# A graph and attention block on one core: ScalarE's weight conversions placed elsewhere, the context in other PSUM banks, and an output product begun at half the context

## The reference

```python
xn = _layernorm(x, axis=-1)
x = x + gnn(xn, edge_index, ...) + mix(xn[None], w_qkv, w_out, b_out, ln_scale)[0]
x = x + ffn(_layernorm(x, axis=-1)[None], ...)[0]

def mix(x, w_qkv, w_out, b_out, ln_scale):            # 8 heads of 64
    q, k, v = jnp.split(jnp.einsum('bnc,cf->bnf', x, w_qkv), 3, axis=-1)
    q = jax.nn.softmax(q, axis=-1)                    # over a head's 64
    k = jax.nn.softmax(k, axis=1)                     # over the nodes
    context = jnp.einsum('bnhd,bnhe->bhde', k, v / N)
    out = jnp.einsum('bhde,bnhd->bhen', context, q / 8)
    out = jnp.einsum('bnf,fc->bnc', heads_joined(out), w_out) + b_out
    return layernorm(out) * ln_scale

def gnn(x, ...):                                      # two layers
    x = prelu(x @ lin_W.T + lin_b)
    agg = jax.ops.segment_sum(x[src], dst, num_segments=n)
    h = prelu((x + agg) @ W1.T + b1) @ W2.T + b2      # then batch norm and relu
```

## Time and profile before

| | us |
|---|---|
| median of 3 runs (530.35 to 535.58) | 530.47 |
| the profiled execution | 531.56 |
| its span, first to last instruction | 529.8 |
| TensorE busy | 478.6 |
| VectorE busy | 323.4 |
| ScalarE busy | 251.7 |
| GpSimd busy | 166.1 |
| mean granted TensorE clock | 0.960 of full speed |

### The profile page before, as it was taken

The page is one execution under the profiler, slowest core; times in us unless marked ns, Lnnn a source line. Parts: engine busy times, 40 slices in busy tenths (PEclk is TensorE's granted clock), DMA queues, the critical chain, the costliest instruction groups (busy, mean ns, idle before and its releaser), DMA issues.

```text
span 529.8 us, 10016 instructions
## 1 busy us (share of the span) xinstructions
PE 478.6 (90%) x3589; PEld 363.3 (69%) x3589; DVE 323.4 (61%) x737; ACT 251.7 (48%) x526; POOL 166.1 (31%) x176
## 2 busy tenths in 40 slices
PE   2989999997997997997999995999999978989893
PEld 1767558875764665664899993668999857866641
DVE  4667698746969855863453536644333376439777
ACT  4778334137451345153235553534336377743344
POOL 1469154003039103033124990002321323303502
PEclk9989999999999989998899997999999957999998
DMA  8602001200102002002100001000000295000015
GB/s 245 188 2 79 1 12 70 81 1 29 51 2 80 2 1 79 2 6 84 74 0 0 2 1 58 1 0 1 0 0 1 83 396 240 1 0 1 1 41 153
DMA packets 5245, 27.42 MB, mean 52 GB/s; under 512 B 1036, under 2 KB 1161, under 8 KB 3544
## 3 DMA queue, kind: packets, MB, share of 16 engines
q1 hardware_dynamic: 5208, 26.92, 14.7%
HBM read 24.36 MB, written 2.56 MB: 51 GB/s over the span
## 4 chain that ended last, share of the span: by engine, by line
PE 73%; DVE 13%; ACT 9%; issue 3%; POOL 1%; DMA 1%; SPq 0%; ACTq 0%; DVEq 0%
PE ps L454 45%; PE ps L612 17%; PE ps L443 5%; PE ps L704 2%; PE ps L508 2%; DVE r L1126 1%; PE ps L440 1%; ACT wslot L756 1%; DVE r L1578 1%; PE ps L518 1%; DVE stat L1148 1%; DVE r L1590 1%; POOL late L1631 1%; DVE r L1568 1%; ACT late L864 1%
## 5 line engine op out<-in xcount | busy, mean ns | idle before, releaser
L454 PE MATMUL ps<-r,wslot 128*128 128x250 f16 x840 | 97.7, 277 | 4.4 <-DVE r L1126 4.3
L454 PEld LDWEIGHTS ps<-r,wslot 128*128 128x128 f16 x840 | 83.1, 100 | 16.9 <-DVE r L1126 5.9
L612 PE MATMUL ps<-late,r 125*128 (+1 forms) x800 | 89.7, 274 | 3.8 <-issue 3.8
L612 PEld LDWEIGHTS ps<-late,r 125*128 125x128 f16 x800 | 78.8, 99 | 15.0 <-issue 4.5
L1639 POOL TENSOR_TENSOR wslot<-stage,wslot 128x512 f16<-128x512 f32 x32 | 39.4, 1261 | 155.7 <-ACT wslot L756 155.7
L454 PE MATMUL ps<-wslot,r 128*125 128x512 f16 x300 | 69.4, 382 | 0.0
L454 PE MATMUL ps<-wslot,late 128*125 128x512 f16 x240 | 56.3, 389 | 6.3 <-DVE late L1418 5.9
L1667 POOL TENSOR_TENSOR late<-ohs,late 128x250 f16<-128x250 f32 x40 | 25.6, 651 | 99.2 <-ACT late L929 99.2
L454 PEld LDWEIGHTS ps<-wslot,r 128*125 128x125 f16 (+1 forms) x300 | 39.4, 137 | 22.2 <-issue 2.3
L454 PE MATMUL ps<-late,wslot 128*128 x480 | 51.5, 270 | 0.0
L454 PEld LDWEIGHTS ps<-wslot,late 128*125 128x125 f16 x240 | 32.8, 140 | 25.2 <-issue 7.5
(11 more groups left out here) (181 smaller groups left out, 745.3 us busy)
## 6 DMA issues: line engine op xcount, KB each, us to landing
late<-in_tv SPq DMA_DIRECT2D x2, 4096.0 KB, 17.5
x<-in_x SPq DMA_DIRECT2D x5, 448.0 KB
out<-r SPq DMA_DIRECT2D x10, 224.0 KB
stage<-in_w_up SPq DMA_DIRECT2D x2, 1024.0 KB, 5.8
stage<-in_w_down SPq DMA_DIRECT2D x2, 1024.0 KB, 4.7
stage<-in_w_lin SPq DMA_DIRECT2D x1, 1024.0 KB, 6.5
stage<-in_w_k SPq DMA_DIRECT2D x1, 1024.0 KB, 4.8
stage<-in_w_q SPq DMA_DIRECT2D x1, 1024.0 KB, 4.9
```

Of the source, the lines that this page charges most:

```text
L454: last = nc.tensor.matmul(out, stat_(hs, b), mov(hm, b), start=start and n == 0, stop=stop and n == 3 * blocks - 1)
L612: last = nc.tensor.matmul(bank("t", m), u_nat[layer][:, p, h, m * 128:(m + 1) * 128], counts(h)[:, chunk], start=(start and h == 0 and p = ...
```

## The change

The arithmetic and the number of instructions stay. What moves:

- ScalarE's weight conversions. "v": from behind the exponentials to between the last two key windows. "out": scaled after q5's exponential, high half after q6's; before, both after v0's window copy. "down0": scaled after v4's window copy, high half after v5's; before, both after v9's. "up1": scaled after v8's window copy, high half at mix tile 0; before at mix tiles 2 and 3. "down1": mix tiles 4 and 5; before 6 and 7.
- The context's PSUM banks: z slots 2 and 3 in place of the two x banks.
- The products m 0 and m 1 wait for the first half of the context only.
- Windows: one of the five of the mix stage now stands between m 1 and m 2 (phase "ctx"), and the other four follow mix tiles 0 to 3 directly; before, five followed tiles 1 to 5.
- The slot of "q" counts as read after q9, not after the last value tile.

```diff
-WINDOWS = {"up0": 4, "k": 6, "v": 10, "mix": 5}
+WINDOWS = {"up0": 4, "k": 6, "v": 10, "ctx": 1, "mix": 4}
...
-    "z": [("qv", 2 * T, "dve", 0)],
+    "z": [("qv", 2 * T, "dve", 0), ("ctx", 2, "dve", 1)],
...
-READER = {"lin": ("t", "lin"), "up0": ("x", "up0"), "k": ("t", "k"), "q": ("z", "qv"), "v": ("z", "qv"), "out": ("n", "m"),
+READER = {"lin": ("t", "lin"), "up0": ("x", "up0"), "k": ("t", "k"), "q": ("z", "qv", QV.index(("q", T - 1)) + 1), "v": ("z", "qv"), "out": ("n", "m"),
...
             for b in range(2):
-                wait_bank(pe, "x", "ctx", b, b)
+                wait_bank(pe, "z", "ctx", b, 2 + b)
...
-            wait_done(pe, "x", "ctx", 2)
             for p in range(KB):
+                wait_done(pe, "z", "ctx", p // 2 + 1)
                 wait_bank(pe, "n", "m", p, p % 2)
...
+                if p == 1:
+                    window("ctx", 0)
...
-                if 1 <= t <= WINDOWS["mix"]:
-                    window("mix", t - 1)
+                if t < WINDOWS["mix"]:
+                    window("mix", t)
...
             for i in range(WINDOWS["k"]):
                 window("k", i)
+                if i == WINDOWS["k"] - 2:
+                    split_weight("v")
...
-            split_weight("v")
...
+                    if t == Q_FIRST - 2:
+                        scale_weight("out")
+                    if t == Q_FIRST - 1:
+                        high_weight("out")
...
                     window("v", t)
-                    if t == 0:
-                        split_weight("out")
-            split_weight("down0")
+                    if t in (4, 5):
+                        (scale_weight if t == 4 else high_weight)("down0")
+                    if t == T - 2:
+                        scale_weight("up1")
...
-                if t in (2, 6):
-                    scale_weight("up1" if t == 2 else "down1")
-                if t in (3, 7):
-                    high_weight("up1" if t == 3 else "down1")
+                if t == 0:
+                    high_weight("up1")
+                if t in (4, 5):
+                    (scale_weight if t == 4 else high_weight)("down1")
...
             dve.wait_ge(k_max, 2)
+            window("ctx", 0)
```

More of the change, by code:

```diff
@@ L1315, in _ @@
             dve.wait_ge(k_max, 2)
+            window("ctx", 0)
             for b in range(2):
-                wait_high(dve, "x", "ctx", b)
+                wait_high(dve, "z", "ctx", b)
                 for hh in range(2):
```

21 lines of the change are left out of this document (11 added, 10 removed).

## The result

The changed kernel took 535.77 us (median of 20 runs, 531.88 to 540.37), the kernel before 532.44 us (20 runs, 530.23 to 535.61). The ratio is 1.0055, with a 95% interval of 1.0037 to 1.0073: the change costs 2.9 us (2.0 to 3.9). This ratio, like those of the experiments, is an estimate over the runs with its interval, and not the quotient of the two medians (here 1.0063). The forecast of 529.6 us was a gain of 0.9 us, and 535.77 lies above its range, which ended at 533.5. Two of the missing 6.2 us are the level of the kernel before, whose median of 20 runs is 532.44 and not 530.47; the rest is the change.

What follows compares the result with a forecast made beforehand. TensorE was taken as the bound, busy 478.6 of 529.8 us. Terms -3.0 - 2.4 + 3.4 - 0.8 + 1.95 gave -0.85, say -0.9 us: 529.6 us from a median of 530.47, range 525.3 to 533.5.

Steps and rivals of the forecast that it cites:

- Step 1: Key stage: "v" converted in ScalarE's idle time; key transposes start at 126.65 instead of 129.69 us, 3.0 us earlier.
- Step 2: "out" converted between the queries: v1's 4.15 us stall goes, less dearer windows beside GpSimd; -2.4 us.
- the walk to v6: Value stage followed window by window: v6 starts on TensorE at 171.75 against 177.19 us, 5.4 us ahead.
- Step 3: "down0" and half of "up1" moved into the value stage: context at 192.75 us, 2.0 of 5.4 us left; +3.4 us.
- as in the mean: Price of a VectorE window beside GpSimd, from instruction times at 157 to 175 us: 4.1 us instead of 2.4.
- Steps 4 and 5: Context to end of mix tiles: -0.8 us up to mix 0, then +1.95 us in the mix tiles.
- Step 4: Context in the z pair, m begun at half: mix 0 15.5 us after the context's start, before 16.3; -0.8 us.
- Step 5: Mix windows without lag: each late, window 2 meets GpSimd's split of "up1" and costs 4.1 us; +1.95 us.
- TensorE's clock falls: Rival: two more falls to half speed behind late windows, turning -0.9 into +2.9 us, 533.4 us; 15 in 100.
- Every window waits in full: Rival: three full GpSimd waits per window, 5.8 us each; v0 to v2, v7, mix 2 add +8.5, 538 us; 3 in 100.

Runs made afterwards that it cites:

- e1: Kernel before with only the conversions of "v" and "out" moved as in the change; 527.83 us, ratio 0.9913 to the kernel before.
- e3: Changed kernel with "down0", "up1" and "down1" converted where they stood before; 524.45 us, ratio 0.9865 to the kernel before.
- e4: Changed kernel with each mix window one tile later again (lag restored); 534.43 us, ratio 1.0042 to the kernel before.
- e10: Changed kernel with GpSimd's split of "up1" held until all windows are built; 535.14 us, ratio 1.0024 to the kernel before.
- e2: Kernel before with only the context's banks, m begun at half, and the ctx and unlagged mix windows changed; 528.11 us, ratio 0.9944.
- e12: The same kernel as e3, run again in another batch; 524.71 us, ratio 0.9843 to the kernel before.
- e5: Changed kernel plus resultless matmuls: 8 before window v7, 5 before the context, 8 before mix window 2; 531.17 us, ratio 0.9992.
- e11: e3 with GpSimd's scaling of the ten query tiles held until all value windows are built; 519.34 us, ratio 0.9744 to the kernel before.
- e7: e6 with GpSimd's split of "down0" held until all ten value windows are built; 527.47 us, ratio 0.9898 to the kernel before.
- e6: e1 with the move of "down0" into the value stage added; 531.28 us, ratio 0.9964 to the kernel before.
- e9: e3 with both halves of "up1" converted at mix tile 0; 531.14 us, ratio 0.9985 to the kernel before.

## Why the prediction was wrong

- **Step 1 (-3.0).** Right: 126.44 for 126.65, no wait, ScalarE at 109.24 for 109.6.
- **Step 2 (-2.4) and the walk to v6.** Right: 171.50 for 171.75, with the dearer windows of v0 to v2 included. e1 gave 4.6 us as time.
- **Step 3 (+3.4): the step that failed.** The mechanism was the one described, and both waits for ScalarE came (1.98 and 3.44 us). But the term was mis-sized: some 6.0 us by the contexts of the seven profiles, 6.7 by after and e3. Of the 2.4 us that the context in after came later than forecast, 1.07 is window v7, for which I took 4.1 us "as in the mean", although a split of four instructions in a row was to lie right across it; it took 5.3, near the 5.8 that I had worked out for full waits. The mean of the earlier trace rows held windows that met the short scaling instructions, some of them in gaps, and was the wrong row for this place; it also left out the 125 x 2048 instruction, which can meet the split too. Another 1.05 is v9 at half clock, for which the term held nothing. Part of this is the execution's luck: in e4, the same program up to there, the window took 4.3 us, the clock did not fall and the context came 0.6 us late; in e10 it came 3.8 us late.
- **Steps 4 and 5 (-0.8 + 1.95).** Step 4 came to 15.9 us for 15.5. Step 5 was mis-assigned and mis-sized. The windows without lag are not all late, and cost no more than the missing fifth window saves (e2: 34.3 us against 34.7); what I had charged to them belongs to the split of "up1" in window 2 and the conversion ahead of it. That window took 4.8 us for 4.1, and the clock fell behind it (1.07 + 3.57 us for 0.62 + 2.75, so 1.27): together 38.2 us for 36.7.
- **The rival "TensorE's clock falls".** In the profile of after it is what happened, twice more than in before: at v9 and at mix tile 3. Its price, -0.9 turned to +2.9, is the measured 2.9. It had 15 in 100, because three late windows in before had passed at full clock, behind waits of 1.3 and 1.6 us that were no shorter than those of after. That row was weak evidence: e3 and e12 show that the same place of one program passes at full clock in one execution and falls in another. The agreement in the sum is partly luck: the two falls gave 2.3 us (1.05 and 1.27), against the rival's 1.9 each, and dearer windows 1.4. The Trainium skill (TensorE: Matmul & The Clock Gate, A second HAM failure mode) describes a kernel in which small pauses between groups of matmuls made the clock swing; here it fell behind pauses of 1.2 and 1.6 us, and stayed up at these two places when matmuls filled them (e5).
- **"Every window waits in full"** had 3 in 100 and was right for one window (5.3 us) and nearly for a second (4.8), not for all. The Trainium skill (SBUF — State Buffer, Who interferes with whom) calls the port pair an exclusive lock held for a whole instruction. Window v7 agrees: the 1 x 16 instruction that takes 0.15 us alone took 1.12, and ended with the split instruction beside it, which itself took 2.14 us for 1.16, because it had met the 125 x 2048 one.
- **The sum.** On the profile's own scale the forecast was 530.7 us; 2.4 at the context, 0.4 to mix 0, 1.5 in the mix tiles and 0.7 in the pause before the gathers make 535.7, and 535.64 was measured. By cause these 5.0 us are 2.3 for the two falls of the clock, 1.4 for the two dearer windows (1.07 and 0.34), 0.7 for the pause and 0.6 for the rest, in which the slower context lies. That pause was 3.5 us in e5, 4.5 in after and 5.6 in e10; what sets it stays open.
- **The range.** The sum was 5 us short on the profile's own scale, and it leaned on a median of 3 runs that lay 2 us below that of 20. On 532.44 the forecast would have been 531.5, still 4.2 us low.

## What to carry to other kernels

When a change moves a conversion on one engine, follow what it sets free as well: here the conversion of "down0" on ScalarE was nearly harmless, and the GpSimd split that follows it, laid across a window that VectorE had to deliver just in time, cost most of what its move lost. Price such a meeting by the worst row of its kind and not by a mean over stages (window v2 of before took 4.7 us, from 158.30 to 162.97, and would have been nearer than 4.1), and add a possible fall of the clock where TensorE then waits in thin work. The cure is to let GpSimd's work start behind the last window (e11, 1.0% faster than the same kernel without it), but count the transfer that waits for it too (e10).

## What the runs showed of the hardware

- **VectorE and GpSimd, both ways.** Beside 128 x 512 splits a window of five instructions took 5.3 and 4.8 us instead of 2.4, and 4.3 where the two lay otherwise (e4). GpSimd paid as well: four split instructions took 5.6 to 6.3 us beside a window, and 4.50 and 4.49 (e7) nearly or wholly without one.
- **The clock falls behind short waits.** After waits of 1.2 us (0.73 + 0.50) and 1.6 us (1.11 + 0.50), each with a late window of small matmuls behind it, the granted clock was 0.50, the lower level, for at least 2 us. It made the tiles behind 1.05 and 1.27 us longer. Matmuls without a use in the wait kept it at 1.00 there, but not ahead of the context, where it fell 3 us behind a pause of 0.74 us although TensorE had been busy since (e5). Waits of the same size in before passed at full clock (161 to 177 us), and whether it falls at one place differs between executions of one program (e3 and e12: 1.45 us longer, of which 0.4 us is left at the next tile).
- **Small matmuls at addresses read from memory.** Sixteen of them took 0.75 to 0.83 us when their window was ready ahead (e7), 1.3 to 1.9 where it was just late (e2, after), and 2.1 to 2.3 after a wait (after, e3, e4, e6, e9, e12).
